# Max tiles of a packed attention kernel: 64 rows of contraction instead of 125, two heads in a pair

## The reference

```
xq  = ada_ln(x1, cond);  xkv = ada_ln(ctx, cond)
q = (xq @ Wq + bq)            -> 16 heads of 8
k, v = split(xkv @ Wkv + bkv) -> 16 heads of 8
scores = q k^T / sqrt(8)      # 256 x 512 a head
out = softmax(scores) @ v
y = x1 + (out @ Wp + bp)
```

## Time and profile before

| | us |
|---|---|
| median of 3 runs | 202.46 (201.9 to 203.8) |
| profiled execution, its own time | 201.29 |
| its span, first to last instruction | 199.5 |
| PE / DVE / ACT / POOL busy | 188.9 / 159.5 / 126.8 / 54.7 |

### The profile page before, as it was taken

The page is one execution under the profiler, slowest core; times in us unless marked ns, Lnnn a source line. Parts: engine busy times, 40 slices in busy tenths (PEclk is TensorE's granted clock), DMA queues, the critical chain, the costliest instruction groups (busy, mean ns, idle before and its releaser), DMA issues.

```text
span 199.5 us, 4395 instructions
## 1 busy us (share of the span) xinstructions
PE 188.9 (95%) x1503; PEld 132.2 (66%) x1503; DVE 159.5 (80%) x478; ACT 126.8 (64%) x280; POOL 54.7 (27%) x75
## 2 busy tenths in 40 slices
...
GB/s 122 304 357 63 8 20 22 28 79 108 110 200 202 7 1 0 18 130 111 12 97 153 70 30 0 6 87 62 74 138 71 110 71 1 1 2 3 5 0 52
DMA packets 12199, 14.65 MB, mean 73 GB/s; under 512 B 1896, under 2 KB 9938, under 8 KB 11602
## 3 DMA queue, kind: packets, MB, share of 16 engines
...
...
## 4 chain that ended last, share of the span: by engine, by line
PE 75%; DVE 14%; ACT 6%; issue 3%; POOL 0%; ACTq 0%; DVEq 0%; POOLq 0%
PE ps L735 67%; PE ps L738 8%; DVE mx L1318 5%; ACT tz L663 2%; ACT tz L672 2%; DVE hT L1241 2%; DVE xn L1177 1%; DVE bias_rows L1060 1%; DVE p L1208 1%; ACT probs L700 1%; DVE qr L1313 1%; POOL rstd L521 0%; DVE qp L1311 0%; DVE nm L1199 0%; ACT p L612 0%
## 5 line engine op out<-in xcount | busy, mean ns | idle before, releaser
L1318 DVE TENSOR_REDUCE mx<-ps 128x1 f32<-128x512 f32 x128 | 82.3, 680 | 4.1 <-PE ps L735 4.0
L700 ACT ACTIVATE probs<-ps 128x512 f32<-128x512 f32 x128 | 65.5, 603 | 6.3 <-PE ps L735 6.2
L735 PE MATMUL ps<-k_st,q_st 125*128 125x512 bf16 x128 | 38.8, 380 | 0.6 <-issue 0.6
L735 PE MATMUL ps<-q_st,k_st 128*128 128x256 bf16 x256 | 35.9, 273 | 0.2 <-DVE mx L1318 0.2
L735 PE MATMUL ps<-probs,vtile 128*32 128x256 f32 x512 | 30.9, 382 | 0.1
L735 PEld LDWEIGHTS ps<-q_st,k_st 128*128 128x128 bf16 x256 | 23.1, 98 | 11.1 <-issue 1.7
L735 PEld LDWEIGHTS ps<-probs,vtile 128*32 128x32 f32 x512 | 15.2, 109 | 12.5 <-ACT probs L700 1.8
L735 PEld LDWEIGHTS ps<-k_st,q_st 125*128 125x128 bf16 x128 | 11.8, 98 | 12.3 <-ACT probs L700 2.9
L663 ACT ACTIVATE tz<-ps,half_b 128x256 f32<-128x256 f32 x28 | 12.0, 474 | 10.0 <-PE ps L735 9.9
L1241 DVE SCALAR_TENSOR_TENSOR hT<-ps,biases,tz 128x256 f32<-128x256 f32 x28 | 12.2, 478 | 4.4 <-ACT tz L672 4.4
L529 POOL TENSOR_TENSOR rstd<-ve,mhalf 128x2 f32<-128x2 f32 x4 | 3.0, 760 | 45.0 <-DVE ve L1284 45.0
...
## 6 DMA issues: line engine op xcount, KB each, us to landing
...
k_scr<-kp SPq DMA_DIRECT2D x12, 128.0 KB, 2.4
...
x_sb<-in_x SPq DMA_DIRECT2D x4, 128.0 KB, 4.4
out<-y_sb SPq DMA_DIRECT2D x4, 128.0 KB, 2.2
```

Of the source, the lines that this page charges most:

```text
L700: A.activation(probs[:, g % 2, j, half * 2 * T:(half + 1) * 2 * T], bank("unit", b, u), ACT.Exp)\
L735: return nc.tensor.matmul(out, lhsT, rhs, start=start, stop=stop)
L1318: V.tensor_reduce(mx[:, b, t, h:h + 1], bank("tile", b, i), AX_X, ALU.max, negate=True)\
```

## The change

**Tiles.** `tile` contracts over 64 partitions instead of 125. The 16 heads are in two sets, x = 0 (heads 0 to 7) and x = 1 (heads 8 to 15). The heads of set 0 have their 72 rows at partitions 0 to 71, those of set 1 at 56 to 127. The rows of set 1 are turned about, so that both sets' outer 64 rows hold the eight larger products of parts. The inner 8 rows are the product of the two third parts, which the maximum now does without; the units use all rows, as before. Consecutive tiles alternate between the sets, same queries, so a tile at partitions 0 to 63 is followed by one at 64 to 127. A group of four heads now has two of each set.

**Maxima.** They stand at the partitions opposite the rows: 125 to 127 for set 0, 0 to 2 for set 1. Each group's maxima are two transfers, `mrow` and `mbow`.

**Staging.** The scratch tensors have a fourth slot, since the third part is written twice (`SLOTS`): 4 `k_out` and 4 `q_out` for each b instead of 3. Each `k_in` issues two transfers of half the size (48 instead of 24 in all), and each `q_in` is followed by a `qb_in` for set 1 (32 instead of 16).

**Unchanged.** Number and size of units, reductions, exponentials and `pv`, and of everything in layer 0.

**Order.** All five lists and the banks are new.

```
+RH = P // 2
+KD = 2 * NP
+SLOTS = ((1,), (2,), (0, 3))
...
-        q_st = sb("q_st", [P, QS, GH, T], BF16)
-        k_st = sb("k_st", [P, KS, HH, S], BF16)
+        q_st = sb("q_st", [P, QS, 2, GH // 2, T], BF16)
+        k_st = sb("k_st", [P, 2, KS, NG // 2, GH // 2, S], BF16)
...
+        def tile_of(i):
+
+            g, n = divmod(i, GH * TC)
+            return g, n % 2, n // 4, n // 2 % 2
...
+                for slot in SLOTS[j]:
+                    sp.dma_start(k_scr[b % 2, slot].rearrange("d h t -> h d t"), kp[:, j, :]).then_inc(s_kscr, 16)
...
+                for x in range(2):
+                    row = x * (P - KR) + j * NP * DH
+                    h = head(half * NG // 2, x, 0)
+                    src = k_scr[b % 2, j + 1 - x, :, h:h + HH // 2, :].rearrange("d h t -> d (h t)")
+                    sp.dma_start(k_st[row:row + NP * DH, x, k_place(b, half)].rearrange("p g i t -> p (g i t)"),
+                                 src.unsqueeze(0).to_broadcast([NP, DH, HH // 2 * S])).then_inc(s_kst[b % 2][half], 16)
+
+            def q_rows(b, g, x):
+                h = head(g, x, 0)
+                src = q_scr[b % 2, 1 - x:1 - x + NP, :, h:h + 2, :].rearrange("s d i t -> (s d) (i t)")
+                row = x * (P - KR)
+                sp.dma_start(q_st[row:row + KR, q_place(b, g), x].rearrange("p i t -> p (i t)"),
+                             src.unsqueeze(0).to_broadcast([NP, NP * DH, GH // 2 * T])).then_inc(s_qst[b % 2][g], 16)
...
+            def maxima(b, g, x):
+                row = (1 - x) * (P - NP)
+                n = NP * GH // 2
+                sp.dma_start(q_st[row:row + NP, q_place(b, g), x], mT[x * n:(x + 1) * n, g, :]).then_inc(s_mrow[g], 16)
...
-                mm(o, q_st[0:P - NP, q_place(b, g), h % GH, t * P:(t + 1) * P],
-                   k_st[0:P - NP, k_place(b, h // HH), h % HH, :]).then_inc(s["tile"], 1)
+                rows_x = slice(x * RH, (x + 1) * RH)
+                mm(o, q_st[rows_x, q_place(b, g), x, j, t * P:(t + 1) * P],
+                   k_st[rows_x, x, k_place(b, g // 2), g % 2, j, :]).then_inc(s["tile"], 1)
...
     "sp": """
-        k_out.3.2 q_out.2.2 k_in.2.0 k_in.2.1 k_in.2.2 q_in.2.0 mrow.1.0 q_in.2.1 q_in.2.2 mrow.1.2 mrow.1.1
+        q_out.2.2 q_in.2.0 qb_in.2.0 q_in.2.1 q_in.2.2 qb_in.2.1 qb_in.2.2 k_in.2.3 mrow.1.3 q_in.2.3 mbow.1.3
```

More of the change, by code:

```diff
@@ L54 @@
[L54 to L88, removed]
@@ new lines @@
+        tile.0.17@5 p0T.3.0@6 rows.0.1@4 tile.0.18@1 tile.0.19@7 tile.0.20@0 tile.0.21@2 pv.0.0@3 tile.0.22@4
+        tile.0.23@6 tile.0.24@1 pv.0.1 tile.0.25@0 tile.0.26@6 tile.0.27@3 eo.2.2@0 unit.0.8@2 unit.0.9@4 eo.2.3
+        unit.0.10@2 unit.0.11@1 unit.0.12@6 eo.2.0@4 tile.0.28@7 tile.0.29@1 unit.0.13@5 unit.0.14@3 unit.0.15@6
+        eo.2.1 tile.0.30@7 tile.0.31@0 hkvT.3@5 s0.3.1@1 rows.0.2@6 kproj.3@5 tile.1.0@0 tile.1.1@7 tile.1.2@3
+        tile.1.3@2 pv.0.2@6 pv.0.3 p0T.3.1@7 tile.1.4@6 tile.1.5@4 unit.0.16@3 unit.0.17@5 tile.1.6@7 tile.1.7@0
@@ new lines @@
+        q_out.0.2 k_in.0.4 k_out.1.1 k_out.1.2 q_in.0.0 qb_in.0.0 q_in.0.3 qb_in.0.3 q_in.0.1 k_in.1.0 k_in.1.1
+        k_in.1.2 qb_in.0.1 k_in.0.5 q_in.0.2 qb_in.0.2 mrow.0.0 mbow.0.0 k_out.2.0 k_out.2.1 q_out.1.0 mrow.0.1
+        mbow.0.1 k_out.2.2 q_out.1.1 q_out.1.2 q_in.1.0 q_in.1.2 qb_in.1.0 k_in.1.3 k_in.1.4 mrow.0.2 mbow.0.2
+        qb_in.1.2 q_in.1.1 q_in.1.3 qb_in.1.3 qb_in.1.1 mrow.0.3 k_in.1.5 mbow.0.3 mrow.1.0 k_out.3.2 mbow.1.0
+        k_out.3.0 k_in.2.0 mrow.1.1 k_out.3.1 k_in.2.1 q_out.2.0 k_in.2.2 mbow.1.1 mrow.1.2 q_out.2.1 mbow.1.2
```

249 lines of the change are left out of this document (140 added, 109 removed).

## The result

The changed kernel takes 229.77 us, median of 4 runs (229.19 to 230.23), where the kernel before takes 202.18 on the same chip: ratio 1.137, 95% interval 1.132 to 1.142. I had predicted 201.4, from 196 to 207. It is 27.6 us slower, outside the range, and in none of my cases. A ratio R is to the kernel before, measured beside the run; a difference written behind it with a plus sign is (R - 1) x 202.3 us.

The account below looks back on a forecast made before the run. TensorE and DVE were taken to bind the middle in turn, TensorE the front and tail. Front +1.8, middle -4.9, tail +2.0 gave -1.1 us: span 198.4, 201.4 us against the median, range 196.0 to 207.0.

Parts of the forecast that it names:

- (g): SP's queue: 64 more transfer issues, 38 us more on top of 47, fit in the span; counted as 0.
- (e): Front: more TensorE work ahead of the first tile, not the transfer, sets its start; +1.8 us, between 0 and 2.5.
- Rival D: SP's queue: maxima transfers stand behind a waiting k_out or q_in, 2 to 3 us a batch; +4, 206.5 us; chance 0.10.
- (a): TensorE, middle: tiles from opposite halves stream together, 68 steps instead of 128, removing 13.1 us.
- Rival E: TensorE, middle: the pairs do not overlap; +3, 205.5 us; chance 0.08.
- (b): TensorE, middle: changes of the array's shape cost about 0.10 us each, 90 instead of 24, 6.6 us more.
- Rival C: TensorE, middle: a change of shape costs 0.25 us instead of 0.10; +3.0, 205.5 us; chance 0.15.
- (c): TensorE, middle: in a run's first pair the second tile waits for its own weight load; 2.3 us in all.
- (d): Middle: DVE's 113.4 us of work takes over from TensorE's 104; with 3.2 idle 116.6 us, 4.9 less.
- (f): Tail: six more TensorE pieces and three shape changes after the last tile; +2.0 us, at least 1.0.

Follow-up runs that it names:

- run 11: Run 9's kernel with each k_in taking one part's 8 rows, each repeated three times in an inner place: 205.66 us, R = 1.017.
- run 1: Kernel before with only its k_in and q_in reading scratch as three copies in the outermost place: 234.58 us, R = 1.155.
- run 3: Changed kernel with POOL's seven memsets held back until the first two normalizations are done: 221.51 us, R = 1.094.
- run 9: Changed kernel, memsets held back, k_in reading part and row as before, q_in repeating each row in an inner place: 207.15 us, R = 1.025.
- run 4: Changed kernel with q scratch holding each part three times, so k_in and q_in need no outermost copies; 32 more q_out: 218.68 us, R = 1.081.
- run 5: Changed kernel with the edits of run 3 and run 4 together: 212.09 us, R = 1.053.
- run 7: Kernel before with each max tile contracted over rows 0 to 63 instead of 0 to 124, no pairs: 211.62 us, R = 1.047.

## Why the prediction was wrong

**The step that failed is (g), "I count 0" for the transfers.** I had counted them, priced their issues at before's 0.38 and 0.80 us and found that 85 us of issues fit. The count was right, the k_in price was not (0.676), and a longer k_in issue cost nothing (run 11). The step never asked how long a transfer takes to land once its access pattern is another. Step (e) took 2.4 us for the landing from the k_scr transfers, whose form did not change, where q_in.0.0 took 3.9 even in the kernel before. Measured in the changed kernel: 6.2 to 7.0 us for the first group and up to 12.3 for a later one. The same form put into the kernel before costs 31.3 us (run 1); taken out of the changed kernel it gives some 14 (runs 3 and 9). Rival D named SP's queue as the place and stopped at +4: place nearly right, mechanism not.

**A second miss had no step at all.** POOL's memsets slide ahead of DVE's first normalizations, 8.3 us (run 3; 6.6 between runs 4 and 5). I had looked at the order of TensorE and SP in the front, not at POOL's against DVE's. These two make 22.6 of the 27.6 us (run 9).

**(a) pairs, right.** The timeline of TensorE in the changed kernel:

```profile
160.99 0.39 PE L773 MATMUL ps<-q_st,k_st 128*128 128x256 bf16 x2
161.31 0.39 PE L773 MATMUL ps<-k_st,q_st 64*128 64x512 bf16 x2
161.63 1.07 PE L773 MATMUL ps<-probs,vtile 128*32 128x256 f32 x16
```

Two tiles take 161.63 - 161.31 = 0.32 us with a change of shape, as one did. The second of a pair starts 4 ns after the first (median of the pairs), and the next pair 0.22 us later. Rival E is refuted.

**(b) changes of shape, right:** a unit before a tile takes 0.32 instead of 0.218 above; 0.10 us each in run 7. Rival C, which needed 0.2, is refuted. **(c) the second half's weights, over-counted:** with 4 ns between the two tiles of a pair, the second load is hidden; my 2.3 us are about 0.

**(d) DVE takes over the middle: right in kind, short in size, and visible only once the transfers were repaired.** In run 9 DVE is busy 114.5 of 120.5 us and waits 1.7 us for tiles (4.0 before). I had 113.4 us of work, let all 4.0 go and kept 3.2 of idling, for 116.6 us; the work is 1.1 us more and 6.0 of idling stayed, so the middle gave 1.0 us instead of 4.9.

**(e) front, +1.8: too small.** The first tile of run 9 starts at 63.9, +5.1, at a granted clock of 0.97 in the front, as in the kernel before. (Run 11, of the same order, was granted 1.00 there and has its first maximum 1.9 us earlier.) Its q had landed at 61.6, so the transfers didn't set it. TensorE's front has 2.2 us more of work, near the 2.0 I had added up; the other 2.9 us are idle time, where I had said that idle time could only absorb work. The longest new wait stands just ahead of the first tile:

```profile
62.95 1.05 PE L774 MATMUL ps<-w2o,hT 128*128 128x128 f32 x8 [1.23 <-DVE hT L1280]
```

In all TensorE waits 2.1 us for `hT` (DVE's result of a hidden layer) and 0.6 for `xn` in this front, against 0.2 in the kernel before. That the new order of `hid` and `eo` costs this is read from the waits; I tried no run on it. **(f) tail, +2.0: right,** +1.7 in the changed kernel and +1.6 in run 9.

Against run 9, where both misses are mended, the sum is off by 205.2 - 198.4 = 6.8 us of span: 3.9 from (d), 3.3 from (e), less 0.4 from (f). No version tried is faster than the kernel before; the nearest, runs 9 and 11, are 2.5% and 1.7% slower. The middle was already within 7 us of DVE's own work and gave 1.0, while front and tail cost 6.7.
